# Layer 0 of a four-layer adapter kernel: batches 2, 4 and 6 with all four input chunks in three split terms

## What is computed

```
w = weight[adapter_ids]                      # [8, 512, 512]
x = x + einsum('bsi,boi->bso', x, w)         # layer 0
x = x + L1(x); x = x + L2(x); x = x + L3(x)  # projections with LoRA terms, a router in L1, a gated MLP in L3
```

## Time and profile before

| | us |
|---|---|
| median of 3 executions | 288.88 (288.87 to 289.06) |
| the profiled execution's own time | 289.18 |
| its span | 287.4 |
| TensorE busy | 278.7 (97%) |
| VectorE busy | 226.8 (79%) |
| ScalarE busy | 158.4 (55%) |
| GpSimd busy | 45.7 (16%) |

### The profile page before, as it was taken

How to read it: one execution, slowest core, us unless ns; L and a number is a source line. 1 busy time by engine, 2 the same in 40 slices (tenths; PEclk the granted TensorE clock), 3 DMA queues, 4 the chain that set the end, 5 groups by cost and what they waited for, 6 DMA issues and landing times.

```text
span 287.4 us, 4499 instructions
## 1 busy us (share of the span) xinstructions
PE 278.7 (97%) x1573; PEld 230.3 (80%) x1573; DVE 226.8 (79%) x341; ACT 158.4 (55%) x256; POOL 45.7 (16%) x67
## 2 busy tenths in 40 slices
PE   6899999999999999999999999999999999999993
PEld 6567878988888778888888888888888888888872
DVE  0698898894746999989786785776789999899890
ACT  2787672412425269776736636646677759940310
POOL 1000000000814502514244044034000000000000
PEclk9999999999999999999999999999999999999999
DMA  5999954008503040030260350420291400000054
GB/s 200 361 400 395 400 189 110 0 0 253 188 0 91 12 130 20 17 131 0 74 219 3 110 182 2 123 97 0 73 375 38 144 1 0 0 2 0 0 161 132
DMA packets 22519, 33.28 MB, mean 116 GB/s; under 512 B 2528, under 2 KB 15328, under 8 KB 22112
## 3 DMA queue, kind: packets, MB, share of 16 engines
q1 hardware_dynamic: 22208, 32.47, 33.6%
q10 hardware_dynamic: 288, 0.52, 0.5%
HBM read 30.89 MB, written 2.10 MB: 115 GB/s over the span
## 4 chain that ended last, share of the span: by engine, by line
PE 84%; DVE 9%; ACT 2%; issue 2%; DMA 2%; SPq 1%; DVEq 0%; ACTq 0%
PE bank L1617 12%; PE bank L1618 12%; PE bank L1619 12%; PE bank L1494 6%; PE bank L1496 6%; PE bank L1495 6%; PE bank L1599 4%; DVE act_lo L963 3%; PE bank L1454 3%; PE bank L1757 3%; PE bank L1471 2%; PE bank L1759 2%; PE bank L1760 2%; PE bank L1478 2%; PE bank L1742 2%
## 5 line engine op out<-in xcount | busy, mean ns | idle before, releaser
L615 ACT ACTIVATE part<-bank 128x512 f32<-128x512 f32 x48 | 28.3, 594 | 39.8 <-PE bank L1619 33.6
L1214 DVE TENSOR_TENSOR part<-bank,part 128x512 f32<-128x512 f32 x44 | 29.1, 681 | 1.4 <-PE bank L1599 1.4
L1139 DVE SCALAR_TENSOR_TENSOR bgu_st<-bgu_st,lo_rows,bgu_raw 128x512 fp32r<-128x512 f32 x22 | 16.8, 800 | 13.4 <-ACT bgu_st L615 13.3
L963 DVE TENSOR_TENSOR w_hl<-w_raw,w_hl 128x512 fp32r<-128x512 f32 x31 | 20.0, 684 | 5.8 <-ACT w_hl L615 5.8
L615 ACT ACTIVATE w_hl<-w_raw 128x512 fp32r<-128x512 f32 x31 | 18.6, 622 | 6.0 <-DMA w_raw<-in_w 5.7
L597 POOL TENSOR_TENSOR s_tmp<-wgu_raw 128x256 f32<-128x256 f32 x11 | 8.4, 763 | 80.7 <-DVE wc_up L963 38.8
L1617 PE MATMUL bank<-xb,wc_gate 128*128 128x512 f32 x48 | 18.9, 394 | 0.0
L1619 PE MATMUL bank<-xb,wc_gate 128*128 128x512 f32 x48 | 18.9, 394 | 0.0
L1618 PE MATMUL bank<-xb,wc_gate 128*128 128x512 f32 x48 | 18.8, 392 | 0.0
L1599 PEld LDWEIGHTS bank<-t_st,bgu_st 128*128 128x128 f32 x88 | 14.7, 188 | 2.8 <-DVE t_st L1204 0.3
L615 ACT ACTIVATE xb<-x_f 128x512 fp32r<-128x512 f32 x14 | 8.8, 626 | 13.5 <-DVE x_f L1084 9.4
(11 more groups left out here) (227 smaller groups left out, 790.2 us busy)
## 6 DMA issues: line engine op xcount, KB each, us to landing
wgu_raw<-in_wgu SPq DMA_DIRECT2D x11, 512.0 KB, 4.3
bgu_raw<-in_bgu SPq DMA_DIRECT2D x40, 128.0 KB, 2.7
w_raw<-in_w SPq DMA_DIRECT2D x16, 256.0 KB, 11.0
w_raw<-in_w SPq DMA_DIRECT2D x3, 1024.0 KB, 6.8
w_raw<-in_w SPq DMA_DIRECT2D x6, 512.0 KB, 10.3
wd_raw<-in_wd SPq DMA_DIRECT2D x4, 704.0 KB, 5.8
out<-x_f SPq DMA_DIRECT2D x8, 256.0 KB, 2.7
x_f<-in_xT SPq DMA_DIRECT2D x6, 256.0 KB, 10.1
```

Source lines behind the costliest of these rows:

```text
L615: return act.activation(dst, src, ACT.Copy)
L963: return dve.tensor_tensor(dst, src, hi.bitcast(F32), ALU.subtract)
L1139: return dve.scalar_tensor_tensor(out=st, in0=st.bitcast(F32), scalar=lo_rows16[:, 0:1], in1=raw, op0=ALU.mult, op1=ALU.add)
L1214: dve.tensor_tensor(dst[:], bank[4 * (n % 2) + b][:], dst[:], ALU.add).then_inc(c_added, 1)
```

## The change

Batches 2, 4 and 6 do chunk 0 in three terms too. `w0_chunks(b)` starts at 0 for them. The split chunk 0 goes to one of two new places, `w0c_hl`, used in turn (`w0_parts` picks the place). Chunk 0's fp32 product falls away in these batches, and with it their increments of `w0_raw_used`; `w0_fp32(b)` counts the remaining ones. Since `x0_high` and `x0_low` work on the chunks that are done in terms, both cover four chunks instead of three. Batches 0, 1, 3, 5 and 7 are computed as before. No load is added and none changes in size.

```diff
+        w0c_hl = [at("w0c_hl0", o_wgu + 16 * KB, [2, D], F32R)]
...
+        w0c_hl.append(at("w0c_hl1", m[0] + 8 * KB, [2, D], F32R))
...
         def w0_chunks(b):
 
-            return range(1 if b else 2, C)
+            return range(0 if b in (2, 4, 6) else 1 if b else 2, C)
 
         def w0_splits(b, c):
 
-            return KC * b - 1 + c if b else c - 1
-
+            return sum(len(w0_chunks(i)) for i in range(b)) + c - w0_chunks(b).start + 1
+
+        def w0_fp32(b):
+
+            return sum(w0_chunks(i).start > 0 for i in range(b + 1))
+
+        def w0_parts(b, c):
+
+            return w0_hl[b % W0_RING][:, :, c - 1] if c else w0c_hl[b // 2 % 2][:]
...
                 if b >= RAW_RING:
-                    sp.wait_ge(w0_raw_used, b - RAW_RING + 1)
+                    sp.wait_ge(w0_raw_used, w0_fp32(b - RAW_RING))
                     sp.wait_ge(w0_lo, w0_splits(b - RAW_RING, C - 1))
...
-                    high(w0_hl[b % W0_RING][:, 0, c - 1], w0_raw[b % RAW_RING][:, c]).then_inc(w0_hi, 1)
+                    high(w0_parts(b, c)[:, 0], w0_raw[b % RAW_RING][:, c]).then_inc(w0_hi, 1)
...
-                    low(w0_hl[b % W0_RING][:, 1, c - 1], w0_raw[b % RAW_RING][:, c],
-                        w0_hl[b % W0_RING][:, 0, c - 1]).then_inc(w0_lo, 1)
+                    low(w0_parts(b, c)[:, 1], w0_raw[b % RAW_RING][:, c], w0_parts(b, c)[:, 0]).then_inc(w0_lo, 1)
...
-                pe.wait_ge(*w0_landed(b, 0))
+                if w0_chunks(b).start:
+                    pe.wait_ge(*w0_landed(b, 0))
                 for c in range(w0_chunks(b).start):
                     ins = pe.matmul(bank[b % 2][:], x_f[:, b, c], raw[:, c], start=(c == 0), stop=False)
-                ins.then_inc(w0_raw_used, 1)
+                if w0_chunks(b).start:
+                    ins.then_inc(w0_raw_used, 1)
                 pe.wait_ge(x0_lo, b + 1)
```

More of the change, by code:

```diff
@@ L489, in _ @@
             adapter3 = ids_of(ids3, agu.shape[0] - 1)
-            sp.wait_ge(w0_raw_used, 5)
+            sp.wait_ge(w0_raw_used, w0_fp32(4))
             sp.wait_ge(w0_lo, w0_splits(4, C - 1))
@@ L1464, in _ @@
                 cols = slice(b * S, (b + 1) * S)
-                raw, hl = w0_raw[b % RAW_RING], w0_hl[b % W0_RING]
+                raw = w0_raw[b % RAW_RING]
                 pe.wait_ge(x_in[b], 16)
@@ L1477, in _ @@
                     pe.wait_ge(w0_lo, w0_splits(b, c))
[L1478 to L1481, removed]
+                    hl = w0_parts(b, c)
+                    pe.matmul(bank[b % 2][:], xa[:, 0, c, cols], hl[:, 0], start=(c == 0), stop=False)
+                    pe.matmul(bank[b % 2][:], xa[:, 0, c, cols], hl[:, 1], start=False, stop=False)
+                    ins = pe.matmul(bank[b % 2][:], xa[:, 1, c, cols], hl[:, 0], start=False, stop=(c == C - 1))
                 ins.then_inc(l0_tm, 1)
```

## The result

The changed kernel takes 290.14 us (median of 5, 289.96 to 290.37) against 288.88. The ratio is 1.0041 (95% interval 1.0030 to 1.0052): slower by 1.26 us, where 1.35 was forecast. The time was forecast well, but two errors stand in it, one of each sign, and most of this part is about them.

A forecast was written before the change was run, and what follows sets the result against it. TensorE, busy 97% of the span, was taken to bound the kernel. Three new waits for VectorE totalling 1.86 us minus 0.51 saved gave 1.35 more, so 290.2 us from a median of 288.88; range 289.5 to 290.9.

The forecast's parts named there:

- the shift should pass through: Behind layer 0: everything is bound to it by TensorE's order, so its 1.35 us delay should reach the end.
- The gain of 0.17 a batch: TensorE, batches 2, 4, 6: three terms take 0.69 us instead of fp32's 0.86, saving 0.51 in all.
- about 0.7, 0.35 and 0.55 forecast: Sign in the trace: TensorE's shown waits for VectorE, in us, ahead of the first term of batches 2, 4, 6.
- The bound that the prediction took from the Trainium skill: VectorE: if operations start only when the pipe is empty, new lows begin up to 0.1 us later, sum near 1.6.
- The sum has 1.35: Layer 0: waits of 0.78, 0.43, 0.65 us minus 0.51 saved; batches 2, 4, 6 lose 0.61, 0.26, 0.48.
- the forecast sign: Sign in the trace: the last adds of layer 0 should come 1.35 us later.
- the restart behind a low: Hand-over from VectorE's low to TensorE streaming at 0.23 us a term: taken as 0.22, allowed ends 0 and 0.31.
- free at: When TensorE could start batches 2, 4, 6: 15.02, 23.86, 33.04 us, the latter two including the forecast shift.
- The first (terms find their data): Rival: waits in layer 0 stay within 0.2 us and TensorE saves 0.51, giving 288.4 us; chance 0.05.
- The second (given back later): Rival: a later wait that does not move with layer 0 returns some tenths, 289.2 us or less; chance 0.09.
- The clock stayed full: Answers the third rival: new TensorE idle gaps lower the clock, one batch's terms take 2.77 more, 293 us; chance 0.02.
- No load of weights was felt: Answers the fourth rival: later-issued loads for batches 6 and 7 add 0.6 us, giving 290.8; chance 0.08.

The follow-up runs named there:

- delay8: Kernel before plus eight more fp32r matmuls behind batch 7 on TensorE, whose result nothing reads; 290.87 us, ratio 1.0066.
- pe_only: Kernel before, but batches 2, 4, 6 run three terms on the previous batch's operands instead of chunk 0's fp32 product, no added split work; 288.60 us, ratio 0.9986.
- fill_gap: Kernel before plus a one-element-a-partition memset on VectorE at the start, into an existing tile so that no tile moves; 288.27 us, ratio 0.9977.
- only2: Changed kernel with only batch 2, instead of 2, 4 and 6, doing chunk 0 in three terms; 289.06 us, ratio 1.0004 against the kernel before.
- only4: Changed kernel with only batch 4, instead of 2, 4 and 6, doing chunk 0 in three terms; 288.77 us, ratio 0.9993 against the kernel before.
- only6: Changed kernel with only batch 6, instead of 2, 4 and 6, doing chunk 0 in three terms; 288.95 us, ratio 0.9997 against the kernel before.
- splits_only: Changed kernel with all its split work, but TensorE does chunk 0 in fp32 as before; 289.87 us, ratio 1.0034 against the kernel before.

## Why the prediction came out as it did

- **What bounds the kernel, and the pass-through.** Right up to the last add. The stretch from layer 1's start to the last add is 243.3 us in both kernels, and in `delay8`, where a delay went through in full. That "the shift should pass through" did not hold for the end.
- **The gain of 0.17 a batch.** Right for batches 4 and 6 (0.17 and 0.15 in `pe_only`), 0.06 in batch 2, where the next low comes first.
- **Where the loss comes from.** Right: one wait ahead of each of the batches 2, 4 and 6, because the fp32 chunk was the cover of VectorE's chain. The list shows 0.68, 0.36 and 0.57, against about 0.7, 0.35 and 0.55 forecast, but this agreement hid the error of the next point. The lows started as worked out (0.60 apart; batch 2's low of chunk 0 at 14.78, forecast 14.89, with the whole run 0.1 earlier). The bound that the prediction took from the Trainium skill, page VectorE: DVE Perf Modes, section The DRAIN you can't avoid, did not show: 22.82, 23.43 and 24.03 are 0.60 to 0.61 apart.
- **The size of the loss in layer 0: the step that failed.** The sum has 1.35; it was 1.85, and the last adds of layer 0 came 1.85 late where 1.35 was the forecast sign. From transposes to transposes the three batches lost 0.76, 0.43 and 0.66 us, where the sum has 0.61, 0.26 and 0.48: each term is short by 0.15 to 0.18. I took the moment at which TensorE was free from the chain of waits (15.02, 23.25, 32.17 in the earlier trace rows) and the restart behind a low from the timeline (19.56 in the earlier trace rows). The two views do not share a zero: the chain dates a matmul behind the drawn end of the one ahead, which lies 0.16 us behind the moment at which the next could have started. In the timeline of the kernel before the same fp32 chunk of batch 4 starts at 23.08, not 23.25:

```profile
23.08 1.02 PE L1471 MATMUL bank<-w_raw,x_f 128*128 128x512 f32 x2
```

  With 14.86, 23.08 and 32.01 from the timeline the waits are 0.94, 0.60 and 0.81, and with 0.51 saved the sum is 1.84, which the trace has as 1.85. The mechanism was right; the term "free at" was mis-read by 0.16 to 0.17, three times. The list of waits leaves the same 0.16 out: the last matmul ahead of batch 2 starts at 14.53 in the changed kernel and is drawn to 14.93, so the list has 0.68 up to 15.61, but behind a ready operand the next would have started at 14.76, 0.85 before.
- **What the sum did not have.** The end got 0.6 to 0.8 us shorter in the median (`fill_gap`; `only2`, `only4`, `only6`). In the changed kernel, with three more instructions on VectorE, the instruction load lies outside the last store as in these. With `fill_gap`'s 0.57, 1.85 becomes 1.28, and 1.26 was measured (interval 0.9 to 1.5). The sum costed VectorE's added instructions as time on the engine and never as length of its stream. That the forecast time was met within 0.1 us is luck: the two errors nearly cancel.
- **The rivals.** The first (terms find their data) is out by the waits. The second (given back later) was named with the wrong place: I looked for a wait of TensorE, and it was behind all computation. Nor is it the delay that shortens the end (`delay8`). The clock stayed full. No load of weights was felt: ScalarE had the high parts ready in all even batches.

## What to carry to other kernels

Work that needs no preparation is a cover for the work that prepares the rest: before replacing a slow first step by a faster one that needs another engine, compare from the trace what that engine has queued between the event that frees it and the new first operand (here 2.0 to 2.9 us in the changed kernel, from the start of the residual add to TensorE's restart) with what the waiting engine still has to do (here 1.2 to 2.1 from the same start). Reordering the preparing engine's queue was worth 0.8 us in layer 0 without touching the matmuls. Take both ends of a wait from one view, and when a difference of some tenths of a per cent is to be explained, split it at two or three fixed events (first matmul, start of a layer, last add, end of span) ahead of looking for a cause.

## What the runs showed of the hardware that I had not expected

- One instruction load of 8 KB or so (11 of them are 0.09 MB on the page) inside the last store goes with 2.8 to 3.3 us for that store instead of 2.3. One more instruction on VectorE, 280 us earlier, moved the load out of it and took 0.6 us off the kernel. One more on ScalarE or eight on TensorE did not.
- Tiles moved by 32 bytes made matmuls that read one of them up to 6 ns longer at the median (394 against 388), 0.7 us over the kernel. The delay arises while the matmuls on `wc_gate` run; moving that tile alone was not tried.
- Behind a wait for a low part in layer 0, TensorE starts 0.14 to 0.15 us after the end of VectorE's operation, in the before and the changed kernel, in `pe_only` and in `splits_only`. It is no constant of the pair of engines: behind `act_lo` (L1757, 128x2560) in the kernel before it starts at 273.52, 0.06 after the end at 273.46.
